# Window attention block on one Trainium2 core: all transposes of a round in one tiled run, projection in full fp32, output product on GpSimd, y1 by row halves, new instruction orders

## The reference

```python
y = roll(layernorm1(x), (-4, -4))                # over the 96 channels of each token
q, k, v = split(windows(y) @ qkv_w.T + qkv_b)     # windows of 64 tokens, 6 heads of 16
a = softmax(q * 16**-0.5 @ k.T + mask)            # mask -100 in the last window row and column
x2 = x + roll(windows_back(a @ v @ proj_w.T + proj_b), (4, 4))
x3 = x2 + gelu(layernorm2(x2) @ w1.T + b1) @ w2.T + b2       # 96 -> 384 -> 96
out = x3 * rsqrt(x3**2 @ gamma.T + beta)
```

## Time and profile before

| | us |
|---|---|
| three runs | 1818.24, 1819.56, 1821.19 (median 1819.56) |
| profiled execution | 1816.74 |
| its span, first to last instruction | 1814.5 |
| TensorE / VectorE / ScalarE / GpSimd busy | 1764.4 / 1677.5 / 1587.7 / 1553.4 |
| chain that ended last: share of TensorE | 95% |
| mean granted TensorE clock | 0.995 of full |

### The profile page before, as it was taken

How to read it: one execution, slowest core, us unless ns; L and a number is a source line. 1 busy time by engine, 2 the same in 40 slices (tenths; PEclk the granted TensorE clock), 3 DMA queues, 4 the chain that set the end, 5 groups by cost and what they waited for, 6 DMA issues and landing times.

```text
span 1814.5 us, 78584 instructions
## 1 busy us (share of the span) xinstructions
PE 1764.4 (97%) x31203; PEld 1344.6 (74%) x31203; DVE 1677.5 (92%) x4637; ACT 1587.7 (87%) x2700; POOL 1553.4 (86%) x1661
## 2 busy tenths in 40 slices
PE   5899999999999999999999999999999999999997
PEld 3677777777777777777777777777777777777774
DVE  5799999999999999999999999999999999999985
ACT  2799999998999899989899999899989989998895
POOL 4488999988898888998898898898888889898883
PEclk9899999999999999999999999999999999999999
DMA  2111222122122122222121221221221221221211
GB/s 57 24 42 39 49 52 42 44 52 44 43 52 45 42 52 42 45 51 43 44 50 36 52 51 37 51 51 36 52 51 35 53 50 34 54 50 33 46 34 27
DMA packets 215143, 81.17 MB, mean 45 GB/s; under 512 B 116118, under 2 KB 214780, under 8 KB 214780
## 3 DMA queue, kind: packets, MB, share of 16 engines
q1 hardware_dynamic: 214218, 76.04, 19.2%
q10 hardware_dynamic: 562, 0.11, 0.0%
HBM read 25.75 MB, written 25.17 MB: 28 GB/s over the span
## 4 chain that ended last, share of the span: by engine, by line
PE 95%; DVE 1%; issue 1%; ACT 1%; DMA 0%; SPq 0%; POOL 0%; POOLq 0%; DVEq 0%; ACTq 0%
PE mm_bank L952 50%; PE score_banks L1013 7%; PE turn_bank L945 7%; PE turn_bank L938 6%; PE mm_bank L986 6%; PE pv_bank L1056 5%; PE score_banks L1033 5%; PE score_banks L1042 3%; PE mm_bank L1069 3%; PE mm_bank L1066 2%; PE score_banks L1021 1%; SPq L373 0%; PE mm_bank L1116 0%; DMA k_block<-k 0%; DMA x_ext<-in_x 0%
## 5 line engine op out<-in xcount | busy, mean ns | idle before, releaser
L452 POOL TENSOR_TENSOR hidden_lo<-hidden,hidden_hi 128x512 fp32r<-128x512 f32 x378 | 480.9, 1285 | 0.0
L539 ACT ACT_TABLE_LOAD x253 | 324.6, 1283 | 4.5
L452 POOL TENSOR_TENSOR attended_lo<-attended,attended_hi 96x512 fp32r<-96x512 f32 x127 | 163.8, 1290 | 111.0 <-DVE attended_hi L834 111.0
L808 DVE TENSOR_REDUCE row_max<-score_banks 128x8 f32<-128x512 f32 x384 | 241.4, 684 | 17.8 <-PE score_banks L1021 9.9
L582 ACT ACTIVATE probs<-shifted 128x512 f32<-128x512 f32 x384 | 236.4, 629 | 20.1 <-DVE shifted L816 13.2
L816 DVE TENSOR_TENSOR shifted<-score_banks,row_max 128x512 f32<-128x512 f32 x384 | 250.8, 680 | 0.0
L615 ACT ACTIVATE hidden<-mm_bank 128x512 f32<-128x512 f32 x381 | 228.6, 600 | 20.5 <-PE mm_bank L952 2.2
L447 POOL TENSOR_SCALAR hidden_hi<-hidden 128x512 fp32r<-128x512 f32 x378 | 228.5, 615 | 4.0 <-ACT hidden L615 3.8
L765 DVE BATCH_NORM_STATS2 stats<-turn_bank 128x6 f32<-128x96 f32 x1024 | 192.8, 250 | 30.2 <-PE turn_bank L938 25.8
L594 ACT ACTIVATE probs_t<-score_banks 128x512 f32<-128x512 f32 x384 | 214.5, 594 | 5.8 <-PE score_banks L1033 4.0
L468 POOL TENSOR_TENSOR x_sq<-x 96x512 f32<-96x512 f32 x126 | 130.7, 1037 | 73.7 <-DVE x L846 66.2
(11 more groups left out here) (144 smaller groups left out, 4815.3 us busy)
## 6 DMA issues: line engine op xcount, KB each, us to landing
x_ext<-in_x SPq DMA_DIRECT2D x128, 192.0 KB, 3.1
k_block<-k SPq DMA_DIRECT2D x768, 32.0 KB
out<-o_ext SPq DMA_DIRECT2D x128, 192.0 KB, 2.7
w_raw<-in_w_t SPq DMA_DIRECT2D x1, 144.0 KB
w<-in_w_t SPq DMA_DIRECT2D x1, 144.0 KB
qkv_raw<-in_qkv_t ACTq DMA_DIRECT2D x1, 108.0 KB
ident_sb<-in_ident SPq DMA_DIRECT2D x1, 64.0 KB, 2.3
q_quadrants<-in_qmask SPq DMA_DIRECT2D x3, 1.0 KB
```

What stands on the lines that cost most here:

```text
L452: nc.gpsimd.tensor_tensor(lo, whole, hi, ALU.subtract).then_inc(is_split, 1)
L539: nc.scalar.preload_act_table_set(name)
L808: nc.vector.tensor_reduce(row_max[:, g, :], group_scores(g), op=ALU.max, axis=AX.X)\
```

## The change

1. All transposes of probs and y_tok of a round go into one function, `turn_run`, on tiles of 64 rows. A full transpose of 128 tokens becomes two half ones, and the two halves alternate between the upper and lower rows of the array. Partners write to different banks: `turn_banks` is now one tensor of two banks, in which both layer norms' normed columns lie, the first 64 tokens of each chunk in bank 0, the others in bank 1. `turn_in` and `split_y2` now wait for both layer norms' copies.
2. The projection is one full fp32 product of `attended`; `round_attended` (VectorE), `rest_of_attended` (GpSimd) and the split of its weights go.
3. `outputs` moves from VectorE to GpSimd.
4. y1 is kept by halves of a window's rows: the GpSimd splits read and write flat, the ScalarE copy becomes two instructions, and k, q and v read their windows in runs of 32 tokens.
5. The lists of all engines but SP are new, and with TensorE's the bank table.

```diff
         MM_ITEMS = [
-            ("sum", ATTEND - 1, log_sum_made, 1, 1),
             ("k", QK, k_ready, 1, 1),
             ("q", QK, q_ready, 1, 1),
             ("den", DIVIDE, log_den_made, 1, 1),
+            ("sum", ATTEND - 1, log_sum_made, 1, 1),
+            ("v", ATTEND, v_ready, 1, 1),
             ("mlp2", SETTLE, x3_ready, 1, 1),
-            ("v", ATTEND, v_ready, 1, 1),
             ("proj", PROJECT, x2_ready, 1, 1),
...
+        def normed_columns(ln):
+            return turn_banks[0:DIM, :, ln * 256:(ln + 1) * 256].rearrange("c r (q t) -> c q r t", t=64)
+        def y1_windows(tile, a):
+            by_window = tile[:, unit_slot(a), :].rearrange("c (h n t) -> c n h t", h=2, t=TOKENS // 2)
+            return by_window[:, half_windows(a), :, :]
...
+            def outputs(A, a):
+                wait_alone(pool, inv_den_ready, A + 1)
+                if has(A - 4):
+                    wait_alone(pool, out_stored[unit_slot(a)], 32 * (A // 4))
+                nc.gpsimd.tensor_tensor(windows_of(o_ext[:, unit_slot(a), :, :], a),
+                                        in_windows(half_of(x3, a)), in_windows(inv_den[:, :]),
+                                        ALU.mult).then_inc(out_ready, 1)
...
                 run(wrap_out, DIVIDE - 1)
-                run(rest_of_attended, PROJECT)
                 run(wrap_x, TURN_IN)
+                run(round_y1, TURN_OUT)
+                run(rest_of_y1, TURN_OUT)
+                run(outputs, DIVIDE)
                 run(square, SETTLE)
                 run(round_squares, SETTLE)
-                run(round_y1, TURN_OUT)
                 run(rest_of_squares, SETTLE)
-                run(rest_of_y1, TURN_OUT)
...
+                    by_window = y1_rows(y1, a)[0:DIM].rearrange("c (n q x) -> c n q x", q=CHUNKS, x=WIN)
+                    for r in range(2):
+                        dst = by_window[:, r * HALF_WINDOWS:(r + 1) * HALF_WINDOWS, :, :]
+                        src = normed_columns(0)[:, :, r, :].rearrange("c q (n x) -> c n q x", x=WIN)
+                        made = nc.scalar.activation(dst, src, ACT.Copy)
...
-                wait(pe, (y_ready[0], y2_split)[ln], A)
+                before = A - (TURN_IN, PROJECT)[ln]
+                wait(pe, y_ready[0], min(before + TURN_OUT + 1, HALVES))
+                wait(pe, y2_split, min(before + MLP + 1, HALVES))
...
+            def turn_run(H):
+                A, norm1, norm2 = H + ATTEND, H + TURN_OUT, H + MLP
+                if has(A):
+                    pe.wait_ge(probs_ready, GROUPS * A + 2)
...
+                    pe.wait_ge(probs_ready, GROUPS * A + 3)
+                if has(norm1):
+                    pe.wait_ge(normed[0], norm1 + 1)
+                if has(norm2):
+                    pe.wait_ge(normed[1], norm2 + 1)
+                for p in range(PAIRS):
+                    if has(A):
+                        made = turn_windows(A, 2, p, 0)
...
+                    if has(norm1):
+                        turn_normed(norm1, 0, p, 1)
...
-                pe.wait_ge(attended_split, A + 1)
+                pe.wait_ge(attended_ready, A + 1)
                 mm_wait("proj", A)
-                in_parts(mm_bank("proj", A)[0:DIM, :], wproj_hi[:, :], wproj_lo[:, :],
-                         attended_hi[:, :], attended_lo[:, :]).then_inc(proj_made, 1)
+                nc.tensor.matmul(mm_bank("proj", A)[0:DIM, :], wproj[:, :], attended[:, :],
+                                 start=True, stop=True).then_inc(proj_made, 1)
...
                 run(scores, ATTEND)
-                run(sum_probs, ATTEND - 1)
-                run(times_v, ATTEND - 1)
                 run(project_k, QK)
                 run(project_q, QK)
-                run(turn_out, MLP, 1)
                 run(denominators, DIVIDE)
+                run(times_v, ATTEND - 1)
+                run(sum_probs, ATTEND - 1)
+                run(project_v, ATTEND)
+                turn_run(H)
                 for n in range(HID_CHUNKS):
                     run(mlp_down, SETTLE, n)
-                run(project_v, ATTEND)
-                run(turn_out, TURN_OUT, 0)
                 run(project, PROJECT)
-                run(turn_two_groups, ATTEND)
                 run(turn_in, TURN_IN, 0)
...
```

More of the change, by code:

```diff
@@ L889, in _ @@
             late(statistics, FINAL, 1)
-            late(outputs, FINAL - 3)
+            last_outputs(FINAL - 3)
             late(normalise, FINAL, 1)
@@ L894, in _ @@
             late(last_squares, FINAL - 1)
[L895 removed]
+            last_outputs(FINAL - 2)
             late(second_residual, FINAL)
             late(last_squares, FINAL)
[L898 to L899 removed]
+            last_outputs(FINAL - 1)
+            last_outputs(FINAL)
         @block.tensor
@@ L937, in turn_in, with turn_windows @@
                         chunk = x2[:, unit_slot(a), c * 128:(c + 1) * 128]
-                    made = nc.tensor.transpose(turn_banks[ln][:, n * DIM:(n + 1) * DIM], chunk,
+                    made = nc.tensor.transpose(turn_banks[:, ln, n * DIM:(n + 1) * DIM], chunk,
                                                ident_sb[0:DIM, 0:DIM])
                 made.then_inc(x_turned[ln], 1)
-            def turn_out(A, a, ln):
-                pe.wait_ge(normed[ln], A + 1)
-                for n, c in enumerate(chunks_of(a)):
-                    made = nc.tensor.transpose(turn_banks[ln][0:DIM, n * 128:(n + 1) * 128],
-                                               y_tok[ln][:, c, :], ident_sb[:, :])
-                made.then_inc(y_turned[ln], 1)
+            def turn_windows(A, m, p, n):
+                half = slice(TOKENS * n, TOKENS * (n + 1))
+                bank, first = (n, (m * PAIRS + p) * TOKENS) if m < 2 else (2, (n * PAIRS + p) * TOKENS)
+                return nc.tensor.transpose(score_banks[:, bank, first:first + TOKENS],
+                                           probs[half, m, p, :, :], ident_sb[half, half])
@@ new lines, in turn_normed @@
+            def turn_normed(A, ln, n, r):
+                half, first = slice(64 * r, 64 * (r + 1)), ln * 256 + n * 64
+                made = nc.tensor.transpose(turn_banks[0:DIM, r, first:first + 64],
+                                           y_tok[ln][half, chunks_of(A)[n], :], ident_sb[half, half])
+                if n == CHUNKS - 1:
+                    made.then_inc(y_turned[ln], 1)
+            def turn_run(H):
+                A, norm1, norm2 = H + ATTEND, H + TURN_OUT, H + MLP
+                if has(A):
+                    pe.wait_ge(probs_ready, GROUPS * A + 2)
+                    for m in range(2):
+                        for p in range(PAIRS):
+                            for n in range(2):
+                                made = turn_windows(A, m, p, n)
+                                if m == 1 and p == PAIRS - 1:
+                                    made.then_inc(probs_turned[n], 1)
+                    pe.wait_ge(probs_ready, GROUPS * A + 3)
[3 more added lines that the diff above has]
+                    pe.wait_ge(normed[1], norm2 + 1)
+                for p in range(PAIRS):
+                    if has(A):
+                        made = turn_windows(A, 2, p, 0)
+                        if p == PAIRS - 1:
+                            made.then_inc(first_windows_turned, 1)
+                    if has(norm1):
+                        turn_normed(norm1, 0, p, 1)
+                for p in range(PAIRS):
+                    if has(norm1):
+                        turn_normed(norm1, 0, p, 0)
+                    if has(norm2):
+                        turn_normed(norm2, 1, p, 1)
+                if has(A):
+                    pe.wait_ge(first_windows_turned, A + 1)
+                for p in range(PAIRS):
+                    if has(norm2):
+                        turn_normed(norm2, 1, p, 0)
+                    if has(A):
+                        made = turn_windows(A, 2, p, 1)
+                        if p == PAIRS - 1:
+                            made.then_inc(probs_turned[2], 1)
```

141 lines of the change are left out of this document (52 added, 89 removed).

## The result

Seven executions of the changed kernel took 1802.85 us in the median (1799.59 to 1811.13), against 1822.99 us (1818.24 to 1826.51, also seven) of the kernel before. The ratio is 0.9897, with a 95% interval of 0.9874 to 0.9920: faster, by about 20 us or 1%. The forecast was 1785, in a range of 1762 to 1816: sign and range are right, the gain is about half of what was forecast. The profiled execution took 1799.59 us, its span 1797.8.

What follows compares the result with a forecast made beforehand. TensorE's own issue bounds the kernel, with VectorE nearly as full. Mean rounds fall from 13.55 to 13.25 us, saving 37 us over 123 rounds; with 3 us given back and the median 2.8 above the profiled execution, 1785, range 1762 to 1816.

Steps and rivals of the forecast that it cites:

- Cost of the turns, the projection, x_ext: TensorE's new work per round: 40 half turns 1.45 us, the full fp32 projection 0.86, the turn of x_ext 0.28.
- the edges: TensorE's switches between whole array and tiles, 0.09 to 0.10 us each; their changes sum to -0.09 a round.
- Rival (c): Half turns of y_tok cost 0.10 us each, set by weight load; round 14.3 us, time 1913; chance 0.04.
- The wait for k's bank: TensorE's denominators wait 0.13 us a round until the k copy empties their bank, making rounds 13.07 and 13.29.
- VectorE's chain: Loop of TensorE's turns to projection, then VectorE's residual to y_tok: 13.12 us, taken as 13.22, setting unmasked rounds.
- few hundredths at each of the five: Estimated extra waits at five links between TensorE and VectorE, raising their loop from 13.12 to 13.22 us.
- B: Time of the 17th transpose in TensorE's turn run, which waits for both y_tok; first_residual starts 4.19 us later.
- Outputs on GpSimd: The moved outputs take 1.28 us on GpSimd and cost nothing, with 1.1 us of cover before the denominators.
- 0.036 per run: Price in us per non-contiguous run on GpSimd, from one-operand y_hi; 64 runs give a ceiling of 3.6 for outputs.
- rival (d): Outputs on GpSimd take their ceiling of 3.6 us, denominators come 1.2 late, round 14.4, time 1925; chance 0.05.
- The sum: Whole program: 123 of 127 rounds save 0.30 us each, 37 us; the profiled 1816.7 becomes 1780, the median forecast 1785.
- I put 0.02 a round, 3 us: Allowance in the rounds for small waits between engines that hold each other within 0.1 us: 0.02 a round, 3 us.

## Why the prediction was right, and where it was wrong

- **Cost of the turns, the projection, x_ext: right.** 40 turns take 1.41, forecast 1.45; projection 0.86; x_ext 0.28; the edges as counted. Rival (c) is out: weights of 128 and 96 columns pass 0.031 us apart in 64-row tiles (40 in 1.41 less 0.16 of drain). The Trainium skill, TensorE: Matmul & The Clock Gate, section LDWEIGHTS (loading the stationary operand), has a load cost its columns over 1.2 in ns; as an estimate by it, loads two side by side would stand 0.040 to 0.053 us apart. The trace disagrees.
- **The wait for k's bank: right in kind, 0.24 for 0.13.** The k copy starts 0.99 behind k's first product, takes 0.60, and the denominators follow 0.14 later where 0.05 was taken. TensorE needed 13.12 and 13.35 for 13.07 and 13.29.
- **VectorE's chain: wrong, and without effect here.** "Which I take", 13.22, was to set the unmasked rounds. It is 12.97: each set of statistics takes 1.78 for 1.83, which makes 13.02, the way from B to the residual is about 0.03 shorter, and the "few hundredths at each of the five" are not there. No wait for y_tok came. That the mean came out, 13.235 for 13.25, is luck: a wait put too low and a chain put too long met in it.
- **Outputs on GpSimd: right**, 1.30 for 1.28, and hidden. But the reason given for y_hi's 1.15 was wrong. "0.036 per run" was no price of runs: it was VectorE's outputs holding GpSimd off. The ceiling of 3.6, and rival (d), rested on that misreading. The change removed the collision, a gain that the prediction didn't see; it lay on a GpSimd that had slack.
- **The sum: here it failed.** "127 rounds; the first four fill the pipeline and I count 123 x 0.30 = 37 us" takes the end for unchanged and every round for undisturbed. In the profiles the rounds themselves saved 35.3 us; the end gave back 10.5, of which 7.3 are the table loads and 1.2 a supply stall, and the excess in the rounds gave back 13.2, of which some 12 are supply stalls; start and filling saved 5.1. That leaves 16.7 of the span. The moved load on ScalarE's list stands in the change (its fifth point), and the prediction doesn't mention it. "I put 0.02 a round, 3 us" was the only term for what disturbs a round, at a quarter of the size, and its reason (engines holding each other) was another one.
- Could the stalls have been seen? The ten of before stand in its trace as gaps with "issue" behind them, 0.3 to 0.9 us each, and the prediction doesn't mention them. What made them 21 us is in part argued: the dense stretch became longer (turns directly behind v), and where a pause cut it in two the stalls went. A pair of rounds also went from 988 instructions to 1034. Modulo 256 that is a drift of 36 a pair before and of 10 now, so a block end that has got into the turn run stays there for a dozen rounds. But that decides which rounds are hit; how many depends on where the count starts: 31 block ends fall into the turn run here, 46 with 144 instructions more at the start.
- Left open: what costs the other 2 us of the new tail, how much of the filling's 2.4 us is the loads', and what decides the size of a stall.

## What to carry to other kernels

Cost a moved step at both ends of the program too: what a loop's body sets up for its first rounds and for the code behind it (a table here) is part of its order. Where TensorE issues hundreds of small instructions in a few microseconds, look for gaps without a releaser and count instructions modulo the size of its program's packets; the count at the start and the drift per round decide which rounds are hit. And before a duration is put down to an operation's shape, look at what the neighbouring engine was doing in these same nanoseconds, and at the same operation where it did not.

## What the runs showed of the hardware that was not expected

- Stalls of TensorE at block ends that fall late into a stretch of about 90 instructions a microsecond, 0.2 to 1.2 us each, in nearly the same rounds in a second profile. In the changed kernel 23 of the 31 block ends in the turn run, and 5 of the 70 in v ahead of it, hold a turn or a product up by over 0.3 us. The Trainium skill, Runtime: NRT & Kernel Launch, section Instruction fetch mechanics, calls the crossing of a 16 KiB boundary, 256 instructions, mostly hidden. Block size and count agree with the trace. So does "mostly" by number, 26 stalls at 261 blocks; but by time these 26 made up most of what the rounds lost.
- An increment of a semaphore on TensorE's queue, waited for by nobody, costs 0.11 us (1.72 us for 16 in a row).
- 1.7 us of idling between full products were followed in nearly every round by a stretch at 1.2 GHz, over a third of the time in all; the same idling ahead of v did not.
